# Expert stage of a two-layer token tower on one core: when residual rows and first weights are fetched

## The reference, cut to what matters

```
h = tok_ref(x, mask, ...)
h = h + attn0(layernorm(h), ...)
h = h + ffn0(layernorm(h), W1, b1, W2, b2, Wr, br)     # 8 experts, the best 2 per token
h = h + attn1(layernorm(h), ...)
h = h + ffn1(layernorm(h), weights_in, weights_out)

# ffn0:
logits = xf @ Wr + br
top_g, top_i = top_k(softmax(logits), 2)
for e in range(8):
    w_e = sum(top_g * (top_i == e))
    y = gelu(xf @ W1[e] + b1[e]) @ W2[e] + b2[e]       # W1[e] 192 x 768, W2[e] 768 x 192
    out = out + w_e[:, None] * y
```

## Time and profile before

| | |
|---|---|
| median of 3 runs | 1827.81 us |
| lowest, highest | 1826.41, 1836.93 us |
| the profiled execution's own time | 1831.29 us |
| its span in the profile | 1829.6 us |
| PE busy over the span | 1645.3 us (90%) |
| DVE, ACT, POOL busy | 1314.9, 1172.6, 659.8 us |
| mean granted clock of PE | 0.97 |

### The profile page before, as it was taken

The page is one execution under the profiler, slowest core; times in us unless marked ns, Lnnn a source line. Parts: engine busy times, 40 slices in busy tenths (PEclk is TensorE's granted clock), DMA queues, the critical chain, the costliest instruction groups (busy, mean ns, idle before and its releaser), DMA issues. The chain is left out here.

```text
span 1829.6 us, 60456 instructions
## 1 busy us (share of the span) xinstructions
PE 1645.3 (90%) x19438; PEld 1502.9 (82%) x19438; DVE 1314.9 (72%) x2962; ACT 1172.6 (64%) x3337; POOL 659.8 (36%) x1326
## 2 busy tenths in 40 slices
PE   2999999999578799999999999579999999999966
PEld 2888888888367699999999999468888888888852
DVE  5888888887585255555555554289999999999855
ACT  2888888888374233333333333389999999999930
POOL 4455555553103133333333332334444444444200
PEclk9999999999788899999999999899999999999978
DMA  4122222222124978888888888377777777777614
GB/s 114 45 65 61 65 61 62 63 61 53 35 65 116 296 231 242 246 243 247 243 246 240 246 244 226 93 217 206 207 208 217 207 214 213 208 209 212 195 41 138
DMA packets 349282, 301.77 MB, mean 165 GB/s; under 512 B 43915, under 2 KB 314335, under 8 KB 349215
## 3 DMA queue, kind: packets, MB, share of 16 engines
q1 hardware_dynamic: 328878, 261.16, 49.6%
q0 software_dynamic: 16032, 37.51, 8.5%
q10 hardware_dynamic: 4304, 2.23, 0.5%
HBM read 207.77 MB, written 93.05 MB: 164 GB/s over the span
## 5 line engine op out<-in xcount | busy, mean ns | idle before, releaser
L1061 ACT ACTIVATE prob<-ps_s,b1s 128x256 f32<-128x256 f32 x426 | 179.2, 472 | 371.3 <-PE ps_s L1030 371.3
L1030 PE MATMUL ps_s<-xhi,w1hi_c 128*128 128x256 f32 x852 | 237.9, 297 | 19.8 <-DVE xhi L1160 18.1
L1030 PE MATMUL ps_s<-xhi,w1lo_c 128*128 128x256 f32 x852 | 228.5, 286 | 0.0
L964 POOL DMA_INDIRECT xs<-zn_d,idx x71 | 93.9, 1323 | 356.5 <-PE ps_t L994 354.0
L1152 DVE CAST w1hi_c<-score 128x768 fp32r<-128x768 f32 x142 | 73.3, 558 | 205.1 <-DMA score<-w1h 204.9
L1005 PE MATMUL ps_v<-probT,prob 128*128 128x192 f32 x852 | 208.3, 326 | 0.0
L1005 PE MATMUL ps_k<-probT,prob 128*128 128x192 f32 x852 | 208.1, 326 | 0.0
L396 PE MATMUL ps_q<-xT,wqk_c 128*128 128x128 f32 x1536 | 196.8, 279 | 1.1 <-ACT kT L643 0.6
L396 PEld LDWEIGHTS ps_q<-xT,wqk_c 128*128 128x128 f32 x1536 | 189.5, 196 | 1.9 <-ACT xT L664 1.0
L1030 PEld LDWEIGHTS ps_s<-xhi,w1hi_c 128*128 128x128 f32 x852 | 165.7, 195 | 22.4 <-issue 20.3
L1030 PEld LDWEIGHTS ps_s<-xhi,w1lo_c 128*128 128x128 f32 x852 | 165.8, 195 | 0.0
(11 more groups left out here) (217 smaller groups left out, 4385.1 us busy)
## 6 DMA issues: line engine op xcount, KB each, us to landing
rel_d<-rpad SPq DMA_DIRECT2D x64, 864.0 KB
relb<-rel_d SPq DMA_DIRECT2D x64, 768.0 KB, 4.7
probT<-w2h SPq DMA_DIRECT2D x71, 576.0 KB
score<-w1h SPq DMA_DIRECT2D x71, 384.0 KB
score<-w1h SPq DMA_DIRECT2D x142, 192.0 KB
ys_d<-ys SPq DMA_DIRECT2D x71, 192.0 KB
tok<-b2h SPq DMA_DIRECT2D x71, 96.0 KB
posb<-pos_w SPq DMA_DIRECT2D x128, 48.0 KB
```

The costliest lines, as they stand in the source:

```text
L964: pool.indirect_dma_start(xs[b][:, s, :], None, zn_d, bass.IndirectOffsetOnAxis(ap=ix[b][:], axis=0)).then_inc(x_ld[b], 16)
L1030: last = pe.matmul(dst, w, x, start=(k == 0), stop=(k == len(terms) - 1))
L1061: last = act.activation(hT[b][:, c, :], ps_s[:, j, (c % 2) * BLK:(c % 2) * BLK + BLK], ACT.Gelu, bias=b1s[b][:, c:c + 1])
```

## The change

The four quarter transfers of `hres` become 64 transfers, one for each column t of `hres` (128 rows of 768 bytes, 96 KB), issued by SP at the head of steps 7 to 70. Their one semaphore is waited for at the start of layer 1 with the full count.

The ages become `w1=0, load=1, h=2, y=3`. The first weights of block n are asked for in step n, the first and second bias and the second weights of block n-1 in that same step. The first weights of block n wait for `split` of block n-2, and no longer for GELU of block n-2. The first bias has a semaphore of its own, on which ACT waits ahead of the GELUs, and still waits for GELU of the block two before it. On SP the order within a step is: `hres` row; wait for GELU of block n-3, first bias of block n-1; wait for `split` of block n-2, three `w1` transfers of block n; wait for the bias addition of block n-3, second weights and second bias of block n-1; store of block n-3. SP reads the expert's number twice in a step. PE, ACT, DVE and POOL do their blocks in the same order as before, one step later.

```diff
-        h1_ld = [sem(f"h1_ld{c}") for c in range(4)]
+        h1_ld = sem("h1_ld")
+        b1_ld = [sem(f"b1_ld{p}") for p in range(2)]
-        ages_d = dict(load=0, h=1, y=2)
+        ages_d = dict(w1=0, load=1, h=2, y=3)
+        ages_sp = dict(ages_d, h1=7)
@@ expert_tensor
-                t = st.n - 1
+                t = st.tile("h")
@@ expert_scalar
+                    act.wait_ge(b1_ld[b], 16 * (st.pair("h") + 1))
@@ expert_vector
-                    dve.wait_ge(w1_ld[b], 64 * (st.pair("h") + 1))
+                    dve.wait_ge(w1_ld[b], 48 * (st.pair("h") + 1))
@@ expert_sync
-                before2 = upto(st.n - 2, NBLK)
-                if isinstance(st.n, int) and 4 <= st.n < 8:
-                    c = st.n - 4
-                    sp.dma_start(hres[:, 16 * c:16 * c + 16, :], hv[:, 16 * c:16 * c + 16, :])\
-                        .then_inc(h1_ld[c], 16)
+                if st.has("h1") and not (isinstance(st.n, int) and st.tile("h1") >= NT):
+                    t = st.tile("h1")
+                    sp.dma_start(hres[:, bass.ds(t, 1), :], hv[:, bass.ds(t, 1), :]).then_inc(h1_ld, 16)
                 if st.has("load"):
                     ex = sp.value_load(etabi[0:1, bass.ds(t, 1)], min_val=0, max_val=E - 1)
-                    after(sp, D_["h_sb"], NH * before2)
+                    after(sp, D_["h_sb"], NH * upto(t - 2, NBLK))
-                    loads = [(w1[b][0], w1h[bass.ds(ex, 1), 0:128, :]), (b1s[b][:], b1h[bass.ds(ex, 1)])]
-                    loads += [(w1[b][1][r:r + D1, :], w1h[bass.ds(ex, 1), 128:, :]) for r in (0, D1)]
+                    sp.dma_start(b1s[b][:], b1h[bass.ds(ex, 1)].rearrange("o k i -> (o k) i")).then_inc(b1_ld[b], 16)
+                if st.has("w1"):
+                    t, b = st.tile("w1"), st.two("w1")
+                    ew = sp.value_load(etabi[0:1, bass.ds(t, 1)], min_val=0, max_val=E - 1)
+                    after(sp, D_["split"], upto(t - 2, NBLK))
+                    loads = [(w1[b][0], w1h[bass.ds(ew, 1), 0:128, :])]
+                    loads += [(w1[b][1][r:r + D1, :], w1h[bass.ds(ew, 1), 128:, :]) for r in (0, D1)]
-                    after(sp, D_["y_sb"], before2)
+                if st.has("load"):
+                    t, b = st.tile("load"), st.two("load")
+                    after(sp, D_["y_sb"], upto(t - 2, NBLK))
-            pipeline(sp, ages_d, body, tiles=NBLK)
+            pipeline(sp, ages_sp, body, tiles=NBLK)
@@ layer 1, vector
-                for c in range(4):
-                    dve.wait_ge(h1_ld[c], 16)
+                dve.wait_ge(h1_ld, 16 * NT)
```

More of the change, by code:

```diff
@@ L1192, in body @@
                     ex = sp.value_load(etabi[0:1, bass.ds(t, 1)], min_val=0, max_val=E - 1)
-                    after(sp, D_["h_sb"], NH * before2)
+                    after(sp, D_["h_sb"], NH * upto(t - 2, NBLK))
                     settle(sp, spare)
-                    loads = [(w1[b][0], w1h[bass.ds(ex, 1), 0:128, :]), (b1s[b][:], b1h[bass.ds(ex, 1)])]
-                    loads += [(w1[b][1][r:r + D1, :], w1h[bass.ds(ex, 1), 128:, :]) for r in (0, D1)]
+                    sp.dma_start(b1s[b][:], b1h[bass.ds(ex, 1)].rearrange("o k i -> (o k) i")).then_inc(b1_ld[b], 16)
[3 more added lines that the diff above has]
+                    after(sp, D_["split"], upto(t - 2, NBLK))
+                    settle(sp, spare)
+                    loads = [(w1[b][0], w1h[bass.ds(ew, 1), 0:128, :])]
+                    loads += [(w1[b][1][r:r + D1, :], w1h[bass.ds(ew, 1), 128:, :]) for r in (0, D1)]
                     for dst, src in loads:
                         sp.dma_start(dst, src.rearrange("o k i -> (o k) i")).then_inc(w1_ld[b], 16)
-                    after(sp, D_["y_sb"], before2)
+                if st.has("load"):
+                    t, b = st.tile("load"), st.two("load")
+                    after(sp, D_["y_sb"], upto(t - 2, NBLK))
                     settle(sp, spare)
```

## The result

The changed kernel takes 1807.62 us (median, 1803.75 to 1820.15) against 1827.68 us for the kernel before (1826.41 to 1836.93); the ratio is 0.9881 with a 95% interval of 0.9848 to 0.9915. The forecast was 1807, 1.1% faster, in a range of 1801 to 1816. The profiled execution took 1803.75 us, the fastest of its four, with a span of 1802.0.

What follows compares the result with a forecast made beforehand. The expert stage was taken as PE-bound from 650 to 1100 and transfer-bound from 598 to 650. Terms -19.8 - 3.0 + 0.5 = -22.3 us put the median at 1805.5 or 1809; forecast 1807, range 1801 to 1816.

Steps and rivals of the forecast that it cites:

- the early loss: Expert stage, blocks 4 to 11: residual quarters queued ahead of first weights lose 19.8 us, which the 64 pieces remove.
- A piece at 0.34 us, hidden: Steady blocks: each piece takes 0.34 us of DMA time, 7.2 us in all, under PE's 7.93, costing nothing.
- the 0.90 that was named as a sign: Whole expert stage: a DMA share flat at 0.90 would show the forecast right.
- The point of decision: Steady blocks: pieces stop being hidden once one costs more than 1.1 us.
- SP's new issue: Each step on SP: one more issue of about 0.5 us and a read fit ahead of an existing wait.
- Rival C: Steps 7 to 70: pieces make DMA the bound, 8.7 us a block, about 1857 us; chance 0.05.
- First weights earlier: Expert stage: asking for w1 earlier raises slack from 0.9 to 5 to 7 us, removing 3.0 us at the end.
- rival A: Stage end and some jitter: late waits stay, keeping 3 to 4 us, 1809 to 1812 us; chance 0.16.
- Rival D: SP too busy to ask for w1 earlier: slack stays 0.9 us, 1813 to 1825 us; chance 0.06.
- The first steps: Step 2: earlier weight loads compete with block 0's second gather, 0.5 us lost, bounds 0 to 2.8.
- The sum: Profiled execution: -19.8 - 3.0 + 0.5 = -22.3 us, own time 1831.3 to 1809.0 us.
- the two assumptions on the median: The profiled execution's 3.5 us above the median are late loads, giving 1809, or lie elsewhere, giving 1805.5.

Runs made afterwards that it cites:

- the second trace of before: The kernel before, unchanged, executed once more for its trace: 1830.95 us, stage 584.6 us.
- three fetches: Changed kernel with each residual piece fetched three times, the extra two into tiles nothing reads: 1805.49 us, stage 564.5 us.
- 384 KB lumps: Residual in 16 transfers of four rows, one every fourth step: 1804.39 us in the changed kernel, 1809.32 us in the kernel before.
- the second pair: Both kernels traced again without edits: stage 563.5 us changed, 584.6 us before; changed median 1807.43 us.
- the run with the extra wait: Changed kernel with SP waiting in step 2 for block 0's gather before block 2's first weights: median 1809.07 us, ratio 0.9874.
- one and three more pieces a step: Changed kernel with each residual piece fetched four and six times, against three: 1858.84 us and 1915.61 us.

## Why the prediction was right

**The bound and the early loss** (19.8 us by the gaps): confirmed. Blocks 4 to 11 keep the period, and the second trace of before gives 17.5 for the same gaps, so the term itself is good to 2.3 us. That the pieces alone bring most of it is shown by the run with the pieces alone, and that they are needed by the run without them.

**A piece at 0.34 us, hidden.** Confirmed by the window from 650 to 1100 with three fetches, where three are hidden; the two added ones took 0.32 us of the DMA engines each. The window of 598 to 1100 moved 255 to 256 GB/s, where the forecast had 255 by bytes; the share is 0.87 and not the 0.90 that was named as a sign. The point of decision, 1.1 us of free time per block or 3.2 pieces, agrees with three hidden and a fourth not, but by luck: what ran out was SP's time, 0.94 us a block at 0.5 a fetch. The prediction fitted SP's new issue in ahead of a wait and never asked how much was left; for one piece that was enough. Rival C is dead at the size of this change. The Trainium skill's rule to batch to 1 MiB ("DMA: Bandwidth & Descriptors", section "Bandwidth") would have left the quarters alone. Here the queue held seven others per block, and 96 KB pieces, 384 KB lumps and the rest ran at the same stage length (564.1, 563.7), so the trace does not bear the rule out at this load.

**First weights earlier** (3.0 us at the end of the stage, slack from 0.9 to 5 to 7): confirmed for the late gaps, 3.0 in the first trace and 2.0 in the second. The late gaps are in all four traces with the late request, and in none of the six with the early one in which transfers or SP are not the bound all along. The prediction took them for late loads that might be jitter; rival A, at 0.16, had them stay. They recur at the same blocks. The slack after can be worked out from the rows of the changed kernel, as an estimate: its h starts at 912.62, less the 3.67 us of DVE is 908.95, and the weights issued at 895.30 land 6.25 to 8.5 us on and 0.3 for the piece, so 4.9 to 7.1 us. The landing itself is in no row. The lumps show the difference: 1.4 us ahead of the weights cost nothing with the early request and 0.1 to 1.2 us with the late one. Rival D falls with it: SP asks in time. The prediction's 1.5 us from the end of GELU to the issue of w1 came out at 1.7 (893.60 to 895.30), and its 1 us for a bias and a read ahead of w1 at 1.4 (893.86 to 895.30).

**The first steps** were the mis-sized term, against the forecast: 0.5 us taken out of 0 to 2.8, and in the first pair of traces 1.9 measured at block 0, 1.4 left at block 1's copy. In the second pair the two are 1.4 and 0.4. Over all traces but that of the run with the extra wait, block 1's copy comes 15.8 to 16.5 us after `row_of` with the late request and 16.6 to 17.5 with the early one, about 1 us more in the mean. The reason given, that the gather is nearly in by then, was wrong; the weights were issued at 562.85 and the gather's second half at 562.98.

**The sum.** Stage: -22.3 forecast, -21.9 and -21.1 measured (586.0 and 584.6 against 564.1 and 563.5). In the second pair it is made up otherwise than forecast, of 17.5 early, 2.0 late, 1.8 at block 51 and 0.4 lost at the start. Of the median: 1807 forecast, 1807.6 and 1807.4 measured. That it hits to 1 us is luck. Between the two assumptions on the median (1805.5 and 1809) the middle was taken without a reason that the traces gave; single executions of the changed kernel run from 1803.75 to 1824.18, and the kernel before has medians of 1827.7 and 1835.4. The profiled execution's own drop of 27.5 us was helped by 5.7 behind the stage. The prediction had named a change of layer 1's time as a sign of being wrong; at this scatter it can't be told.

## What to carry to other kernels

A transfer that nobody needs for hundreds of microseconds must not stand ahead of those that the next block needs: cut it so that what is queued ahead costs less than the slack of the tightest load, and place it where the DMA engines and the engine that issues both have free time in each step. Work out that slack as a time, from issue to the last moment that hurts nobody, for every load in the queue; asking earlier for one of them only passes the wait on. Count the issuing engine's own time as well: here it, and not the DMA engines, was used up first. Read its waits before adding transfers; once there are none, each transfer added lengthens the step.

## What the runs showed of the hardware that was not expected

- 281 GB/s at a share of 0.95 were moved over 450 us while PE stayed the bound. With one and three more pieces a step it fell to 267 and 266 GB/s at shares of 0.90 and 0.89, and SP no longer waited for anything: eleven issues, in part slowed, and the reads filled its step of 8.70 us.
- With a quarter of the residual in the queue, SP itself stood still at its next issue: 4.36 us in the earlier trace rows and 3.6 to 5.8 at the other three quarters, 4.4 to 6.6 us for a bias of 3 KB in the run with the quarters back, against 0.34 us.
- First weights came late at the same blocks in four traces. A copy at line 1055 follows h of the block before it, so the gaps at the copies of blocks 51 or 52, 68 and 70 belong to the weights of blocks 50 or 51, 67 and 69. In the first trace those of 67 are the row of 1110.94 in the earlier trace rows, the last that SP issues in its loop, and those of 69 the second behind it. What delays them was not tried; the earlier request hides it.
